# The pipeline of an adaLN block: its loop of five passes against nineteen bodies written out

## Chip, cores and metric

The kernel runs on one core of a Trainium2 chip. The metric is device time in microseconds (us) of one execution; for the kernel before three were timed, with a median of 753.84 us (753.83 to 755.56).

## What is computed

16 images (B) of 512 tokens by 128 channels, all in f32. Each goes through sliding-window attention with 16 heads of 8 channels, a window of 32 tokens to each side, and then a mixture of 8 experts, two of them chosen per token, with a shared expert beside them. Both halves are modulated by vectors that come from a condition.

```python
mod = (silu(c) @ wmod).reshape(16, 6, 1, -1)
sa, ca, ga, sb, cb, gb = (mod[:, i] for i in range(6))   # ga, gb kept away from 0 by 0.25
h = layernorm(x) * (1 + ca) + sa
x = x + ga * attention(h)          # q, k, v, softmax in a band of +-32, o
h = layernorm(x) * (1 + cb) + sb
x = x + gb * ffn(h)                # softmax router, top 2 of 8, silu(x w1) * (x w3) @ w2, and a shared expert
```

## The kernel before

**Tiling.** One image is the unit of work. Its tokens lie in the free dimension, 512 columns, and the 128 channels on the partitions. Products that need more precision than one fp32r pass gives are made from three matmuls of a high and a low part (`exact3`, L1157 to L1159). Attention takes 16 blocks of 32 queries; a block's four head groups are four matmuls of 96 keys (`scores`, L1214), then comes the row maximum on DVE (`maximum`, L883, tile nmx), the exponential with its sum on ACT (`probabilities`, L680, tile p), a transpose on DVE (`turn_p`, L900, tile pt) and the product with v on PE (`values`, L1237). Queries and keys reach the layout that `scores` needs by way of HBM: SP writes q_scr and k_scr and reads them back in two halves for each image (`load_half`, L320 for q, L328 for k), the second of which is needed at score block 8. The row sums go by way of r_scr (`spread_sums`, L350 and L354), and the router's weights by way of s_scr (`spread_scores`, L334 and L343, tile sbc, four transfers of 512 KB). The experts are nine rounds of two `exact3` products into ps_A and ps_B, a tanh on ACT (L723), two steps on DVE (L980 and L989), and the product with w2 (`down`, L1282); POOL makes the low parts of the experts' inputs (L494, L500).

**The pipeline.** Every engine (SP, POOL, ACT, DVE, PE) has one function `body(b, par)`, in which the steps of four images are interleaved by hand: image b's attention, image b+1's layer norm and projections, image b-1's output projection and router, and the experts of images b-2 and b-3. `has(b, back)` leaves out the steps of images that don't exist, at the two ends. `par` is b's parity and chooses buffers. There are 19 bodies, b from 0 to 18. The engines have no common barrier: each runs through its bodies by itself, and semaphores whose counts rise through the whole run tie them together.

`pipeline` (L232) issues the bodies. b = 0 to 3 and b = 14 to 18 are written out, with b an integer. b = 4 to 13 are a loop of five passes with two bodies in each, on every engine; b is a register expression there. In the loop each wait for a semaphore needs its count worked out by a register operation (REGISTER_ALU or ISA in the lists below, ALU_OP and FUSED_REGOPS in the trace), and every DMA to or from an image's own rows has an address from a register. At the end of a pass each engine adds to its counter and does a compare-and-branch (both at L236).

Of the kernel before, what the change touches and what calls it, by code (L numbers as in the profile page):

```python
# [28 lines left out]
B, S, D = 16, 512, 128  # L29
# [28 lines left out]
def build(nc, x, w13, w2, wqkv, wo, gate, bias, borow, cT, wmod, out):  # L58
    ctx = ExitStack()
    with ctx:  # L60
# [170 lines left out]

        def pipeline(eng, body):  # L232

            for b in range(4):
                body(b, b % 2)
            with eng.Fori(2, B // 2 - 1) as i:  # L236
                body(2 * i, 0)
                body(2 * i + 1, 1)
            for b in range(B - 2, B + 3):
                body(b, b % 2)  # L240

        def has(b, back, first=0):
# [17 lines left out]
        def _(sp):  # L260
# [120 lines left out]
            def body(b, par):  # L381
# [18 lines left out]
                if has(b, 1):  # L400
                    spread_scores(b - 1)

            pipeline(sp, body)
            sp.wait_ge(out_d, 16 * B + 16)


        @block.gpsimd
        def _(pool):
# [149 lines left out]
            def body(b, par):  # L558
# [45 lines left out]
                if has(b, 2):  # L604
# [3 lines left out]
                    scaled_low(b - 2, 7, par)  # L608

            pipeline(pool, body)  # L610


        @block.scalar
        def _(act):
# [119 lines left out]
            def body(b, par):  # L734
# [73 lines left out]
                if has(b, 2):  # L808
                    scaled_high(b - 2, 7, par)
                    scaled_high(b - 2, 8, par)  # L810

            pipeline(act, body)


# [627 lines left out]
```

## Time and profile before

| | |
|---|---|
| median of 3 runs | 753.84 us (753.83 to 755.56) |
| profiled execution | 756.55 us |
| its span, first to last instruction | 754.7 us |
| mean granted clock of TensorE over the span | 0.908 |
| PE busy | 672.0 us, 89% |
| ACT busy | 611.9 us, 81% |
| DVE busy | 580.9 us, 77% |
| POOL busy | 540.7 us, 72% |
| queue of the kernel's own DMAs (q1) | 62.8% of 16 engines |
| instruction queues (q8, q14) | 24 and 72 packets |

The busy shares are of the span and can lie over each other. The granted clock is a share of 2.4 GHz, and it stands either at 1.0 or at 0.5. The profiled execution took 2.7 us more than the median of the timed ones; sums in what follows are made against its own time.

### The profile page before, as it was taken

Reading aid. Unit: us, or ns where it says so; the run is one execution under the profiler, and the core shown is the slowest. Engines: PE = TensorE matmul, PEld = TensorE weight load, DVE = VectorE, ACT = ScalarE, POOL = GpSimd, SP = SyncE. Lnnn points to the kernel's source line nnn. Section 1 sums busy time; section 2 is a strip of 40 time slices with the busy share of each in tenths; the row PEclk is TensorE's granted clock in tenths of the full one; section 3 lists DMA queues with packets and bytes.
Section 4 is the critical chain, followed back from the end, with each engine's and each line's share of the span. In section 5 each row is a group of like instructions: output and inputs, shape, how many; then the busy total and the mean of one; then the engine's idle time right before and its main releaser. Section 6 shows DMA issues by size and latency. Waiting matters only on the chain.

```text
span 754.7 us, 20381 instructions
## 1 busy us (share of the span) xinstructions
PE 672.0 (89%) x5934; PEld 566.4 (75%) x5934; DVE 580.9 (77%) x1541; ACT 611.9 (81%) x2602; POOL 540.7 (72%) x564
## 2 busy tenths in 40 slices
PE   2278889989999889998899979998999999989886
PEld 1167677878888768877788768877888888877665
DVE  5456667978899759986899858987799899886453
ACT  4287879988999869997799959997799999885432
POOL 4430417896888768895688858896688888778784
PEclk9655557999999989999799979999799999999999
DMA  4746686767776856778476846878567878624120
GB/s 145 188 104 169 175 206 176 183 190 178 213 189 183 214 163 172 211 196 213 117 184 197 215 139 174 210 188 202 128 189 192 211 196 220 185 45 146 30 102 15
DMA packets 193856, 127.48 MB, mean 169 GB/s; under 512 B 110640, under 2 KB 170848, under 8 KB 193632
## 3 DMA queue, kind: packets, MB, share of 16 engines
q1 hardware_dynamic: 193760, 126.50, 62.8%
q14 instruction: 72, 0.59, 0.2%
q8 instruction: 24, 0.39, 0.2%
HBM read 96.29 MB, written 30.17 MB: 168 GB/s over the span
## 4 chain that ended last, share of the span: by engine, by line
PE 48%; DMA 15%; issue 9%; SPq 8%; POOL 7%; ACT 6%; DVE 6%; DVEq 0%; POOLq 0%; ACTq 0%
PE ps_s L1214 11%; DMA k<-k_scr 10%; PE ps_Y L1282 9%; PE ps_O L1237 5%; SPq L320 4%; ACT p L680 4%; PE ps_A L1157 3%; DMA r_scr<-rst 3%; PE ps_A L1158 2%; PE ps_A L1159 2%; PE ps_B L1157 2%; PE ps_B L1158 2%; PE ps_B L1159 2%; POOL xl L500 2%; POOL xs L494 2%
## 5 line engine op out<-in xcount | busy, mean ns | idle before, releaser
L680 ACT ACTIVATE p<-ps_s,nmx 128x96 f32<-128x96 f32 x1024 | 333.4, 351 | 59.7 <-DVE nmx L883 47.1
L680 ACT ACTIVATION_READ_ACCUMULATOR p<-ps_s,nmx 128x1 f32 x1024 | 222.2, 217 | 0.0
L1214 PE MATMUL ps_s<-k,q 128*128 128x96 f32 x1024 | 170.9, 302 | 48.9 <-DMA k<-k_scr 25.8
L1214 PEld LDWEIGHTS ps_s<-k,q 128*128 128x128 f32 x1024 | 151.8, 215 | 76.9 <-ACT p L680 37.9
L883 DVE TENSOR_REDUCE nmx<-ps_s 128x4 f32<-128x384 f32 x256 | 138.2, 548 | 70.7 <-PE ps_s L1214 61.9
L500 POOL TENSOR_TENSOR xl<-xs,xh 128x512 fp32r<-128x512 f32 x128 | 163.5, 1283 | 28.2 <-ACT xh L702 27.3
L494 POOL TENSOR_TENSOR xs<-h,sbc 128x512 f32<-128x512 f32 x128 | 163.8, 1285 | 5.0 <-DMA sbc<-s_scr 4.7
L1282 PE MATMUL ps_Y<-w2s,g 128*128 128x128 f32 x1152 | 162.2, 289 | 0.6 <-DVE g L989 0.6
L1282 PEld LDWEIGHTS ps_Y<-w2s,g 128*128 128x128 f32 x1152 | 149.3, 200 | 5.1 <-DVE g L989 0.8
L900 DVE STREAM_TRANSPOSE pt<-p 128x384 f32<-128x384 f32 x256 | 135.9, 558 | 2.8 <-ACT p L680 1.1
L980 DVE SCALAR_TENSOR_TENSOR th<-th,ps_A 128x512 f32<-128x512 f32 x144 | 97.7, 678 | 46.7 <-ACT th L723 46.6
L723 ACT ACTIVATE th<-ps_A 128x512 f32<-128x512 f32 x144 | 87.9, 610 | 26.8 <-PE ps_A L1159 25.6
L989 DVE TENSOR_TENSOR g<-th,ps_B 128x512 f32<-128x512 f32 x144 | 98.1, 682 | 12.7 <-PE ps_Y L1282 6.6
L702 ACT ACTIVATE xh<-xs 128x512 fp32r<-128x512 f32 x128 | 81.3, 645 | 22.9 <-POOL xs L494 22.0
L1157 PE MATMUL ps_A<-xh,w13h 128*128 128x512 f32 x144 | 71.2, 494 | 6.6 <-DVE th L980 5.0
L1237 PE MATMUL ps_O<-pt,vd 128*32 128x96 f32 (+2 forms) x2304 | 66.6, 252 | 0.7 <-POOL vd L472 0.7
L472 POOL TENSOR_TENSOR vd<-vt,bmask 128x1024 f32<-128x1024 f32 x32 | 60.6, 1894 | 0.1
L1157 PE MATMUL ps_B<-xh,w13h 128*128 128x512 f32 x144 | 59.2, 411 | 0.2
L1237 PEld LDWEIGHTS ps_O<-pt,vd 128*32 128x32 f32 x2304 | 48.2, 116 | 14.3 <-issue 6.0
L1158 PE MATMUL ps_A<-xh,w13l 128*128 128x512 f32 x144 | 58.6, 407 | 0.0
L1159 PE MATMUL ps_A<-xl,w13h 128*128 128x512 f32 x144 | 58.5, 406 | 0.0
L1158 PE MATMUL ps_B<-xh,w13l 128*128 128x512 f32 x144 | 58.3, 405 | 0.0
(119 smaller groups left out, 935.8 us busy)
## 6 DMA issues: line engine op xcount, KB each, us to landing
sbc<-s_scr SPq DMA_DIRECT2D x64, 512.0 KB, 5.5
k<-k_scr SPq DMA_DIRECT2D x64, 384.0 KB
q<-q_scr SPq DMA_DIRECT2D x128, 96.0 KB
k<-k_scr SPq DMA_DIRECT2D x32, 336.0 KB
q_scr<-qh SPq DMA_DIRECT2D x32, 256.0 KB, 2.5
k_scr<-kh SPq DMA_DIRECT2D x32, 256.0 KB, 2.9
xt<-x SPq DMA_DIRECT2D x16, 256.0 KB, 6.0
q_scr<-ql SPq DMA_DIRECT2D x16, 256.0 KB, 2.5
```

Source lines behind the costliest of these rows:

```text
L494: nc.gpsimd.tensor_tensor(xs[:, n % 2], h2[:, par], sbc[:, n - 1], ALU.mult).then_inc(xs_d, 1)
L500: nc.gpsimd.tensor_tensor(xl[:, n % XRING], src, xh[:, n % XRING].bitcast(F32), ALU.subtract).then_inc(xl_d, 1)
L680: last = nc.scalar.activation(p[:, n % PRING, gg, :], ps_s[:, n % 2, MK * gg:MK * gg + MK], ACT.Exp, bias=nmx[:, n, gg:gg + 1], accum_out= ...
L883: nc.vector.tensor_reduce(nmx[:, n, :], ps_s[:, n % 2, 0:ACC].rearrange("p (g k) -> p g k", g=HG), AX.X, ALU.max, negate=True).then_inc(mx ...
L900: nc.vector.transpose(pt[:, n % TRING].rearrange("p g r q -> p (g r q)"), p[:, n % PRING].rearrange("p g k -> p (g k)")).then_inc(tr_d, 1)
L980: nc.vector.scalar_tensor_tensor(th[:, par], th[:, par], 1.0, ps["A"][:], ALU.add, ALU.mult).then_inc(v_d, 1)
L989: nc.vector.tensor_tensor(g[:, par], th[:, par], ps["B"][:], ALU.mult).then_inc(g_d, 1)
L1157: mm(dst, wh, xh, start=True, stop=False)
L1158: mm(dst, wl, xh, start=False, stop=False)
L1214: last = mm(ps_s[:, n % 2, MK * gg:MK * gg + MK], heads[:, h, gg, nl], k4[:, h, gg, :, MB * nl:MB * nl + MB], start=gg == 0, stop=gg == HG ...
L1237: last = mm(ps["O"][r, MB * n0:MB * n0 + MB * cnt], vd[:, kb, gg].rearrange("p j d -> p (j d)"), src, start=kb == 0 and run is runs[0], st ...
L1282: last = mm(ps["Y"][:, QB * a:QB * a + QB], g[:, par, QB * a:QB * a + QB], w2s[:, e, :], start=n == 0 and a == 0, stop=n == NX - 1, skip_g ...
```

## The change

`pipeline` becomes a plain loop at build time. The bodies 4 to 13 get an integer b like the others, so their waits have constant counts and their DMAs constant addresses, and the branches and register operations of the loop are gone. What each body computes and the order of its steps stay as they are.

```diff
         def pipeline(eng, body):

-            for b in range(4):
-                body(b, b % 2)
-            with eng.Fori(2, B // 2 - 1) as i:
-                body(2 * i, 0)
-                body(2 * i + 1, 1)
-            for b in range(B - 2, B + 3):
+            for b in range(B + 3):
                 body(b, b % 2)
```

The file is five lines shorter, so L883 of before is L878 in the changed one, and so on.

DVE at the end of the loop's second body, before (nmx, th, g, pt: the maximum, the two expert steps, the transposed probabilities):

```order
L900 STREAM_TRANSPOSE pt<-p 128x384 [waits pv_mm,exp_d] x3
L883 TENSOR_REDUCE nmx<-ps_s 128x4 [waits sc_mm]
L979 REGISTER_ALU
L980 SCALAR_TENSOR_TENSOR th<-th,ps_A 128x512 [waits th_d]
L900 STREAM_TRANSPOSE pt<-p 128x384 [waits pv_mm,exp_d]
L989 TENSOR_TENSOR g<-th,ps_B 128x512 [waits y_mm,v_d,b_mm]
L236 REGISTER_ALU
L236 COMPARE_AND_BRANCH
```

and at the head of the loop's first body, to which the branch goes:

```order
L236 ISA
L883 TENSOR_REDUCE nmx<-ps_s 128x4 [waits sc_mm]
L888 ISA
L891 RECIPROCAL rs<-acc 128x64 [waits rst_mm,exp_d]
L838 ISA
L842 BN_STATS l_st<-xt 128x6 [waits x_in]
L842 BN_STATS l_st<-xt 128x6 x3
L882 REGISTER_ALU
L883 TENSOR_REDUCE nmx<-ps_s 128x4 [waits sc_mm]
```

The same place in the changed kernel, the end of an odd body and the head of the next:

```order
L895 STREAM_TRANSPOSE pt<-p 128x384 [waits pv_mm,exp_d] x3
L878 TENSOR_REDUCE nmx<-ps_s 128x4 [waits sc_mm]
L975 SCALAR_TENSOR_TENSOR th<-th,ps_A 128x512 [waits th_d]
L895 STREAM_TRANSPOSE pt<-p 128x384 [waits pv_mm,exp_d]
L984 TENSOR_TENSOR g<-th,ps_B 128x512 [waits y_mm,v_d,b_mm]
L878 TENSOR_REDUCE nmx<-ps_s 128x4 [waits sc_mm]
L886 RECIPROCAL rs<-acc 128x64 [waits rst_mm,exp_d]
L837 BN_STATS l_st<-xt 128x6 [waits x_in]
L837 BN_STATS l_st<-xt 128x6 x3
L878 TENSOR_REDUCE nmx<-ps_s 128x4 [waits sc_mm]
```

The compute instructions are the same and in the same order. The branch, its addition and the register operations are gone, and the head of the next body stands right behind the end of the one before.

ACT at the end of the loop's second body, before (xh: an expert's input rounded; p: exponentials):

```order
L680 ACTIVATE p,acc<-ps_s,nmx 128x96 x3
L698 REGISTER_ALU
L702 ACTIVATE xh<-xs 128x512 [waits b_mm,xs_d]
L698 REGISTER_ALU
L702 ACTIVATE xh<-xs 128x512 [waits b_mm,xs_d]
L236 REGISTER_ALU
L236 COMPARE_AND_BRANCH
```

and in the changed kernel:

```order
L675 ACTIVATE p,acc<-ps_s,nmx 128x96 x3
L697 ACTIVATE xh<-xs 128x512 [waits b_mm,xs_d] x2
L675 ACTIVATE p,acc<-ps_s,nmx 128x96 [waits tr_d,mx_d]
L675 ACTIVATE p,acc<-ps_s,nmx 128x96 x3
L718 ACTIVATE th<-ps_A 128x512 [waits g_d,a_mm]
```

Here too the next body's exponentials follow without a branch.

## Rows read from the trace of the kernel before

**Rows 1.** The page: busy time of PE and others, and the granted clock by slices.

```profile
PE 672.0 (89%) x5934; PEld 566.4 (75%) x5934; DVE 580.9 (77%) x1541; ACT 611.9 (81%) x2602; POOL 540.7 (72%) x564
...
PEclk9655557999999989999799979999799999999999
```

**Rows 2.** Windows of bodies 3 to 14: start:end, length, busy us (x instructions), PEclk, DMA share, GB/s.

```profile
144.60:186.50 41.90, 39.50 (x375) 33.93 (x371) 35.22 (x96) 37.51 (x164) 33.13 (x35) 0.96 0.67 187
186.50:225.02 38.52, 38.16 (x374) 32.48 (x371) 35.05 (x96) 37.37 (x164) 33.41 (x35) 1.00 0.78 204
225.02:266.70 41.68, 38.50 (x371) 32.39 (x371) 35.48 (x96) 38.22 (x166) 33.38 (x35) 1.00 0.72 188
266.70:311.28 44.58, 41.44 (x371) 35.41 (x371) 34.77 (x95) 36.68 (x159) 32.54 (x35) 0.92 0.67 175
311.28:350.39 39.11, 38.06 (x374) 32.55 (x370) 34.94 (x96) 37.60 (x166) 33.10 (x35) 1.00 0.74 199
350.39:396.80 46.41, 42.17 (x375) 35.88 (x371) 35.35 (x96) 37.27 (x162) 33.14 (x35) 0.89 0.62 168
396.80:435.28 38.48, 38.09 (x374) 32.56 (x371) 34.92 (x96) 37.58 (x166) 33.09 (x35) 1.00 0.73 202
435.28:482.43 47.15, 42.84 (x374) 36.47 (x371) 35.63 (x96) 37.58 (x164) 33.47 (x35) 0.89 0.62 166
482.43:521.78 39.35, 38.00 (x370) 32.50 (x371) 34.71 (x96) 37.56 (x164) 32.77 (x35) 1.00 0.77 198
521.78:567.86 46.08, 42.39 (x374) 36.08 (x370) 35.33 (x96) 37.27 (x162) 33.15 (x35) 0.89 0.63 170
567.86:606.21 38.35, 38.10 (x375) 32.56 (x371) 34.91 (x96) 37.47 (x166) 33.09 (x35) 1.00 0.79 203
606.21:644.05 37.84, 37.84 (x374) 32.51 (x370) 34.98 (x96) 37.09 (x164) 33.08 (x35) 1.00 0.75 198
```

**Rows 3.** Records of line L236, 264 to 271 us: ns min/median/max, first and last start.

```profile
L236 DVEq COMPARE_BRANCH  x1: 63/63/63, 265.8 to 265.8; - x1
...
L236 ACTq COMPARE_BRANCH  x1: 45/45/45, 267.0 to 267.0; - x1
...
L236 DVEq FUSED_REGOPS  x1: 74/74/74, 268.6 to 268.6; - x1
L236 ACTq FUSED_REGOPS  x1: 59/59/59, 269.4 to 269.4; - x1
```

**Rows 4.** Timeline of DVE behind the third branch: start, us, instruction [idle before].

```profile
444.00 0.56 DVE L883 TENSOR_REDUCE nmx<-ps_s 128x4 f32<-128x384 f32 x1 [4.17 <-PE ps_s L1214]
```

**Rows 5.** Timeline of ACT behind the third branch.

```profile
441.32 0.34 ACT L680 ACTIVATE p<-ps_s,nmx 128x96 f32<-128x96 f32 x1 [4.59 <-issue]
```

**Rows 6.** Timeline of PE, in body 5 and behind the third branch.

```profile
248.62 0.65 PE L1214 MATMUL ps_s<-k,q 128*128 128x96 f32 x4 [2.53 <-DMA k<-k_scr]
...
442.77 1.09 PE L1214 MATMUL ps_s<-k,q 128*128 128x96 f32 x4 [3.15 <-ACT p L680]
```

**Rows 7.** Windows behind the first and the third branch, columns as in rows 2.

```profile
275.00:281.90 6.90, 6.79 (x24) 6.11 (x25) 4.91 (x9) 4.60 (x21) 4.92 (x6) 0.51 0.36 82
...
442.30:452.50 10.20, 9.30 (x35) 8.43 (x36) 6.86 (x17) 6.84 (x33) 5.42 (x8) 0.50 0.18 45
```

**Rows 8.** DMA queues, 275 to 600 us and then 606 to 644 us: packets, MB, share.

```profile
q14 instruction: 39, 0.32, 0.3%
...
q8 instruction: 3, 0.05, 0.6%
```

**Rows 9.** Timeline of SP in bodies 5 and 14: start, us, instruction.

```profile
226.86 1.76 SPq L343 DMA_DIRECT2D sbc<-s_scr  x4
...
236.99 0.57 SPq L354 DMA_DIRECT2D rt<-r_scr  x1
...
606.40 1.76 SPq L343 DMA_DIRECT2D sbc<-s_scr  x4
...
614.75 0.57 SPq L354 DMA_DIRECT2D rt<-r_scr  x1
```

## The prediction

> **What bounds the kernel now.** I read the page first, then a table of windows, one for each body of the pipeline (a body's window runs from the first score matmul of one image, L1214, to that of the next), then the branch records, the timeline behind a branch, the clock, and last the DMA queues.
>
> The page has PE at 89% of the span, and a granted clock with dips to 7 and 8 tenths that come back again and again in the middle of the run [rows 1]. Those dips are what the reader should take from it: something regular interrupts TensorE there.
>
> The windows say what. Bodies 4 to 13 are the five passes of the loop; body 3 and body 14 are written out. Body 14 lasts 37.84 us with PE busy 37.84, so it is bound by PE at the full clock. The odd bodies of the loop last 38.35 to 41.68 us with PE busy 38.00 to 38.50. The even bodies 6, 8, 10 and 12 last 44.58, 46.41, 47.15 and 46.08 us, at a mean clock of 0.92 or 0.89 [rows 2]. Body 4 is even too and lasts 38.52 us, at clock 1.00: it is the one even body of the loop that is entered from the code above and not over the branch back. So the long bodies are those behind a taken branch, not the even ones as such.
>
> The records of line L236 show the gap. At the end of the first pass DVE's compare-and-branch starts at 265.8 us and takes 63 ns, and its next record, the first instruction of the loop's body, starts at 268.6; ACT's pair is 267.0 and 269.4 [rows 3]. Nothing is waited for there: these are register operations. Behind the third branch ACT stands 4.59 us with the releaser "issue", DVE stands 4.17 us once more before its second maximum, and PE then waits 3.15 us for ACT's exponentials [rows 4 to 6]. DVE's 4.17 is put down to PE's scores, but ACT's own late start shows how little was moving. Right behind that the granted clock is 0.50, the lower of its two levels (1.2 of 2.4 GHz), for 10.20 us, and 0.51 for 6.90 us behind the first branch [rows 7]. TensorE had been standing before each of these stretches.
>
> Where the instructions come from is in the DMA view. Between 275 and 600 us the queue named instruction q14 has 39 packets, and PE's kind of queue, q8, has no row at all. In body 14 there are three packets of q8, 0.6% of 16 engines over 38 us, which is 3.6 us or 1.2 us for each packet [rows 8]. I read this as: the two bodies of the loop stay loaded for PE, while DVE and ACT must have theirs brought back after a branch, and stand until it has come.
>
> **The change, part by part.**
>
> *The four taken branches go.* The loop has five passes and so four branches back, one just ahead of the start of each of the bodies 6, 8, 10 and 12; the fifth falls through. The four bodies behind them sum to 44.58 + 46.41 + 47.15 + 46.08 = 184.22 us. A body without a branch before it costs PE's work plus PE's waits. PE's work: bodies 4, 5, 7, 9, 11, 13 and 14 have 38.16, 38.50, 38.06, 38.09, 38.00, 38.10 and 37.84 us, mean 38.11. PE's waits, window less busy: 0.36, 3.18, 1.05, 0.39, 1.35, 0.25 and 0.00, mean 0.94 [rows 2]. Together 39.05, four times 156.2. Gain 28.0 us. It divides into PE's idle time, 3.14 + 4.24 + 4.31 + 3.69 = 15.4 us, less 4 x 0.94, and PE's longer busy time, 41.44 + 42.17 + 42.84 + 42.39 less 4 x 38.11 = 16.4 us, which is matmuls at half the clock.
>
> That the price lies behind the branch and not in it can be weighed against a rule. The branch record itself is 63 ns on DVE and 45 ns on ACT [rows 3]. The Trainium skill, "Advanced Engine Details and Errata", Control Flow Timing, gives a compare-and-branch about 108 ns and names no other cost; by that rule alone four branches are worth 0.4 us on an engine, and the time would stay near 753.4 us. The Trainium skill, "Runtime: NRT & Kernel Launch", Instruction fetch mechanics, says the other thing: a taken branch to a target outside the loaded window has to fetch it, and the engine stands. The trace agrees with the second, by 2.4 and 2.7 us between branch and next record.
>
> *The other six bodies of the loop* sum to 38.52 + 41.68 + 39.11 + 38.48 + 39.35 + 38.35 = 235.49 us; six times 39.05 is 234.3. Gain 1.2 us. There is no direct gain in them.
>
> *Register operations and separate waits go.* In the loop each wait count is made by a register operation before the instruction; with constants it isn't. The loop's odd bodies need 38.00 to 38.50 us of PE, body 14 without register operations 37.84 [rows 2]. Some tenths for a body at most, and PE's queue runs ahead of PE. I put it at nothing; the 0.27 us between 38.11 and 37.84 in ten bodies, 2.7 us, is kept for the low end. Below nothing it can't well be, since no instruction is added. On SP the same holds: issues of its DMAs with constant addresses are of the same length in body 14 (1.76 us for four of sbc) as in body 5 [rows 9].
>
> *What is added is code to be brought in.* Eight more bodies of instructions on every engine. For PE the loop had none to bring between 275 and 600 us; written out it has three blocks a body, as body 14 shows, some 30 in ten bodies. In body 14 the blocks land and PE is busy 37.84 of 37.84 us, so I cost them at nothing: what hides them is that they are fetched ahead. Their traffic is 0.6% of the DMA engines.
>
> **Sum.** 419.7 us of loop become 390.5: 29.2 us less. The profiled execution took 756.55 us (span 754.7 and 1.85 around it), so 727.3 by its own account. The median of the runs is 753.84, 2.7 less than the profiled one, and gives 724.6. I take the middle, **726.0 us**.
>
> **What is late next** is the second half of k. In body 5 PE waits 2.53 us at score block 8 for k from k_scr [rows 6]. SP had put the four transfers of sbc at 226.86, the row sums could be read back only at 236.99, 10.1 us later, and k was issued behind that. In body 14 the same steps are 606.40 and 614.75, 8.4 us, and PE waits for nothing [rows 2, 9]. The order on SP isn't changed, so this wait stays and decides how much of the gain is kept.
>
> **The rivals.**
> 1. *The k wait settles at its worst.* Bodies 4 and 5, the only two full ones in a row at full clock without a branch before either, average 40.10 us. Ten of them are 401.0: a gain of 18.7 and 737.9 us from the profiled time, 735.1 from the median. For it: bodies 3 and 5 both have it, at 41.9 and 41.68 [rows 2]. Against: bodies 9, 13 and 14 hardly have it. Chance 0.22.
> 2. *No k wait at all.* Ten bodies like body 14, 378.4 us: a gain of 41.3, 712.5 to 715.3 us. Only one body in seven was like that. Chance 0.08.
> 3. *Nothing changes*, because the branch costs only its own record, or because the stall behind it is one that the pipeline has at the turn of each pair of bodies for another reason. Four times 63 ns less, 753.6 us. Body 4 and body 14, even and without a stall, speak against it. Chance 0.03.
> 4. *Slower: PE must wait for its own blocks.* If PE came to the end of a block before the next had landed, each of 30 blocks would cost it the 1.2 us that a packet takes, 36 us, or more in a full DMA queue, and the stops would pull the clock down as they do now: 756.5 - 29.2 + 36 = 763 us. It decides from 1.0 us a block. For it: on PE the loop is the better form as it stands, no fetch in 325 us. Against: three blocks in body 14 with no idle time. Chance 0.03.
>
> **The numbers.** My own forecast has 0.64. The range must take in rival 1 and most of the likely case's spread: its ends are 737.9, where the k wait is at its worst, and 715.3, where it is gone, measured from the median. So 715 to 738. A difference of 0.3%, 2.3 us, is what a measurement of this kernel can tell from none; the forecast and rivals 1 and 2 are all far beyond it. Faster 0.94, same 0.03, slower 0.03.
>
> **What the profile of the changed kernel would show.** No record of line L236's branch. No idle time of ACT or DVE put down to issue in the middle of the run, and no stretch at clock 0.50 between 180 and 700 us, so slices of 9 in the PEclk row. Bodies 4 to 13 of 38 to 41 us each, the odd and the even alike. A mean clock up from 0.908, PE's busy time down by some 16 us to 656, 90% of the new span. Some 24 more packets in q8. What would prove me wrong: bodies 6, 8, 10 and 12 still over 44 us; PE idle for issue at even distances; or waits for k of over 3 us, which would say that DMA has become the bound.

## The result, and the profile after

The changed kernel takes 748.7 us (median of 20 runs, 741.6 to 756.3) and the kernel before 755.2 (median of 20, 746.7 to 761.3). The ratio is 0.9917, 95% interval [0.989, 0.9945]: a gain of some 6.5 us in place of 29. The profiled executions are 746.85 us after and 756.55 before, spans 745.1 and 754.7, 9.6 us apart. Ratios here and below leave out executions over 1.5% slower than the fastest of their kernel, medians keep them (three of the changed kernel's 20, and one of 2311 us among the six of the kernel that spreads 16 KB over 16 engines).

From the page of the changed kernel, beside [rows 1]; the last two lines are the instruction queues (packets, MB, share), which were 24 and 72 packets:

```profile
PE 660.5 (89%) x5934; PEld 558.9 (75%) x5934; DVE 581.2 (78%) x1541; ACT 613.0 (82%) x2602; POOL 541.2 (73%) x564
...
PEclk9996557999989999999999999999999999999999
...
q8 instruction: 47, 0.77, 0.5%
q14 instruction: 53, 0.43, 0.2%
```

The dips in the middle of PEclk are gone at this resolution, and so is every record of the branch. q8, the queue that fills when PE is written out, has 23 packets more. (11868 matmuls and weight loads and 321 semaphore instructions of PE over 47 packets are 259 each; in what follows a block is one 16 KB packet of q8, by this estimate some 256 instructions.) Here are the windows of bodies 4 to 14, with the columns of [rows 2]:

```profile
186.73:230.08 43.35, 41.07 (x375) 35.51 (x371) 35.21 (x96) 37.64 (x164) 33.07 (x35) 0.92 0.69 181
230.08:268.85 38.77, 37.89 (x375) 32.50 (x371) 35.07 (x96) 37.41 (x164) 33.10 (x35) 1.00 0.78 201
268.85:308.89 40.04, 38.15 (x375) 32.40 (x371) 35.17 (x96) 37.45 (x164) 33.07 (x35) 1.00 0.71 196
308.89:348.26 39.37, 38.19 (x374) 32.51 (x370) 35.07 (x96) 37.62 (x164) 33.13 (x35) 1.00 0.76 199
348.26:388.72 40.46, 37.99 (x375) 32.51 (x371) 35.75 (x96) 38.02 (x166) 33.69 (x35) 1.00 0.72 194
388.72:428.20 39.48, 37.90 (x370) 32.50 (x370) 34.52 (x95) 36.94 (x161) 32.59 (x35) 1.00 0.76 198
428.20:467.24 39.04, 37.90 (x374) 32.50 (x370) 35.09 (x96) 37.41 (x164) 33.09 (x35) 1.00 0.79 201
467.24:509.83 42.59, 39.48 (x374) 33.91 (x370) 35.19 (x96) 37.51 (x164) 33.15 (x35) 0.96 0.71 184
509.83:551.85 42.02, 39.79 (x375) 34.08 (x371) 35.22 (x97) 37.64 (x164) 33.11 (x35) 0.96 0.72 186
551.85:591.39 39.54, 37.96 (x374) 32.50 (x371) 35.61 (x96) 37.94 (x166) 33.66 (x35) 1.00 0.76 198
591.39:633.14 41.75, 39.50 (x370) 33.99 (x370) 34.68 (x96) 37.20 (x161) 32.62 (x35) 0.96 0.65 180
```

The even bodies are no longer the long ones. But the ten bodies 4 to 13 sum to 404.7 us against 419.7 before and 390.5 in the forecast, and body 14, which was written out in both kernels, went from 37.84 to 41.75. The four bodies behind a branch lost 22.7 us (184.22 before, 161.56 now); bodies 4, 5, 7, 9, 11 and 13 went from 235.49 to 243.10 us and gave a third of that back.

PE's waits, first in the changed kernel, 186.7 to 591.4 us, then in the kernel before, 186.5 to 606.2 us (who waited for whom: us, times, longest):

```profile
PE ps_s L1209 <- DMA k<-k_scr: 17.6, 11, 3.1
PE ps_B L1152 <- DVE g L984: 0.2, 1, 0.2
```

```profile
PE ps_s L1214 <- ACT p L680: 13.7, 8, 3.1
PE ps_s L1214 <- DMA k<-k_scr: 6.7, 9, 2.5
PE ps_M L1247 <- DVE rs L891: 1.5, 3, 0.5
```

The waits for ACT behind a branch, 13.7 us, are gone as forecast. The waits for k went from 6.7 to 17.6 us: one at score block 8 of each body, and a short one at the start of body 9. The four bodies with the longest waits (4, 11, 12 and 14, 2.1 to 3.1 us) are those with a mean clock under 1.00. The half clock that [rows 7] showed behind the branches stands behind these waits too, here in bodies 14 and 4:

```profile
616.00:619.00 3.00, 3.00 (x14) 2.81 (x13) 2.35 (x5) 2.94 (x14) 3.00 (x4) 0.51 0.91 348
...
209.50:216.00 6.50, 6.50 (x28) 6.21 (x29) 3.81 (x7) 3.93 (x19) 6.50 (x6) 0.50 0.54 207
```

How a wait for k comes about can be followed on SP. In body 14 of the changed kernel (beside body 14 in [rows 9]):

```profile
588.60 0.32 SPq L329 DMA_DIRECT2D s_scr<-smT  x1
593.12 1.75 SPq L338 DMA_DIRECT2D sbc<-s_scr  x4
596.33 1.44 SPq L345 DMA_DIRECT2D r_scr<-rst  x2
600.93 0.57 SPq L349 DMA_DIRECT2D rt<-r_scr  x1
...
604.87 3.05 SPq L323 DMA_DIRECT2D k<-k_scr  x3
```

PE then stands at score block 8:

```profile
614.04 0.65 PE L1209 MATMUL ps_s<-k,q 128*128 128x96 f32 x4 [2.25 <-DMA k<-k_scr]
```

In the kernel before, the two rows of body 14 that [rows 9] lacks are:

```profile
603.94 0.34 SPq L334 DMA_DIRECT2D s_scr<-smT  x1
...
611.15 1.46 SPq L350 DMA_DIRECT2D r_scr<-rst  x2
```

From the s_scr write (588.60) to sbc are 4.5 us, before 2.5. The r_scr write goes out 4.94 us into the body in both kernels, since it waits for ACT's row sums. It takes 4.6 us from there to rt, before 3.6, so rt goes out at 9.5 us into the body instead of 8.5 and k at 13.5 instead of 12.5. The changed kernel's PE goes on at 22.6 us, having stood for 2.25; before, it passed the same block at 20.35 us without a wait. So k's own landing was later by more than the 1.0 us that its issue had lost.

### The profile page after: what moved, and what is told of

Read it like the earlier page. It is cut to its first block, busy times and chain, and to the rows that moved or that the text cites. A ratio compares the mean times of both kernels' runs of the same rounds, so it can differ in the third digit from the quotient of the medians.

```text
span 745.1 us, 18977 instructions
## 1 busy us (share of the span) xinstructions
PE 660.5 (89%) x5934; PEld 558.9 (75%) x5934; DVE 581.2 (78%) x1541; ACT 613.0 (82%) x2602; POOL 541.2 (73%) x564
## 4 chain that ended last, share of the span: by engine, by line
PE 42%; DMA 22%; SPq 13%; POOL 8%; issue 6%; ACT 5%; DVE 3%; POOLq 0%; DVEq 0%; ACTq 0%
DMA k<-k_scr 15%; PE ps_s L1209 11%; PE ps_Y L1277 10%; SPq L315 8%; DMA r_scr<-rst 6%; PE ps_O L1232 5%; ACT p L675 4%; SPq L323 3%; PE ps_A L1152 3%; POOL xl L495 3%; POOL xs L489 2%; PE ps_M L1260 2%; PE ps_A L1153 2%; PE ps_A L1154 2%; PE ps_B L1152 2%
## 5 line engine op out<-in xcount | busy, mean ns | idle before, releaser
L675 ACT ACTIVATION_READ_ACCUMULATOR p<-ps_s,nmx 128x1 f32 x1024 | 215.7, 211 | 0.0
L1209 PE MATMUL ps_s<-k,q 128*128 128x96 f32 x1024 | 167.2, 297 | 54.1 <-DMA k<-k_scr 42.2
L1209 PEld LDWEIGHTS ps_s<-k,q 128*128 128x128 f32 x1024 | 147.6, 210 | 81.4 <-DMA k<-k_scr 50.2
L878 DVE TENSOR_REDUCE nmx<-ps_s 128x4 f32<-128x384 f32 x256 | 138.0, 548 | 67.4 <-PE ps_s L1209 64.0
L1232 PE MATMUL ps_O<-pt,vd 128*32 128x96 f32 (+2 forms) x2304 | 64.9, 247 | 0.0
L1154 PE MATMUL ps_B<-xl,w13h 128*128 128x512 f32 x144 | 57.2, 397 | 0.0
```

What stands on the lines that cost most here:

```text
L675: last = nc.scalar.activation(p[:, n % PRING, gg, :], ps_s[:, n % 2, MK * gg:MK * gg + MK], ACT.Exp, bias=nmx[:, n, gg:gg + 1], accum_out= ...
L878: nc.vector.tensor_reduce(nmx[:, n, :], ps_s[:, n % 2, 0:ACC].rearrange("p (g k) -> p g k", g=HG), AX.X, ALU.max, negate=True).then_inc(mx ...
L1154: return mm(dst, wh, xl, start=False, stop=True)
L1209: last = mm(ps_s[:, n % 2, MK * gg:MK * gg + MK], heads[:, h, gg, nl], k4[:, h, gg, :, MB * nl:MB * nl + MB], start=gg == 0, stop=gg == HG ...
L1232: last = mm(ps["O"][r, MB * n0:MB * n0 + MB * cnt], vd[:, kb, gg].rearrange("p j d -> p (j d)"), src, start=kb == 0 and run is runs[0], st ...
```

## Experiments

All ratios are to the kernel before, which ran on the same chip beside them, with 95% intervals. The first question is which engine's code made the difference. `pipeline` got a switch, so that each engine could keep the old loop or be written out:

```diff
-        def pipeline(eng, body):
+        def pipeline(eng, body, loop=False):
...
-            pipeline(pe, body)
+            pipeline(pe, body, loop=True)
```

**PE alone in the loop** (the diff above; it is the kernel "with PE alone in the loop" below, and the one that the others are held against).

> PE alone keeps the loop of five passes, the other four engines are written out. Theory A (the 16 KB instruction blocks that PE fetches in written-out code, 1.0 to 1.3 us each and three per body, hold up the short transfers s_scr, r_scr and k): no such block between 260 and 600 us, the k waits of PE fall back from a mean of 2.0 us per body to about 1, and the time is 5 us or more below the changed kernel's 748.7, that is a ratio to the kernel before of 0.985 or less. Theory B (the chain over sbc, r_scr and k is just as long as PE's work once no engine stalls, whatever is fetched): same as the changed kernel, ratio 0.99 to 0.993, k waits still 2 us. If PE's branch costs something of its own, the even bodies are longer than the odd ones.

726.3 us, ratio 0.9599 [0.9548, 0.9651]. First the windows of its bodies 6, 9 and 13 and the sum over bodies 6 to 13; then PE's waits in bodies 4 to 13, and q8 on its page:

```profile
269.53:308.25 38.72, 37.88 (x375) 32.50 (x371) 35.05 (x96) 37.35 (x163) 32.99 (x35) 1.00 0.76 201
...
385.91:423.84 37.93, 37.91 (x375) 32.51 (x371) 34.98 (x96) 37.15 (x164) 33.08 (x35) 1.00 0.77 205
...
539.73:577.36 37.63, 37.63 (x375) 32.60 (x371) 35.10 (x96) 37.04 (x164) 33.04 (x35) 1.00 0.76 207
sum 307.83, PE 303.19 PEld 260.15 DVE 280.55 ACT 298.41 POOL 264.41; mean PE 37.90 PEld 32.52 DVE 35.07 ACT 37.30 POOL 33.05
```

```profile
PE ps_s L1218 <- DMA k<-k_scr: 8.8, 8, 2.3
```

```profile
q8 instruction: 24, 0.39, 0.2%
```

The eight bodies 6 to 13 take 307.8 us, 38.5 each, where the changed kernel takes 322.5. The waits for k are half of what they were, and of their 8.8 us 4.2 lie in bodies 4 and 5, the pass in which q8 still has packets. This is the size that the prediction had given for the whole change: 30 us less than the 756.7 of its own comparison. Writing PE out as well costs 22 us (748.7 against 726.3), 24 by the ratios.

**PE alone written out** (`loop=True` for the other four).

> PE alone is written out, the other four engines keep the loop. Theory A: the stalls of DVE and ACT behind the branch stay and PE's blocks come in addition, so slower than the kernel before by 2 to 6 us, ratio 1.003 to 1.008. Theory B: the time of the kernel before, ratio 0.998 to 1.002. In both the even bodies 6, 8, 10 and 12 keep their 44 us and more.

767.0 us, ratio 1.015 [1.0088, 1.0212]: slower than before by 10 us, more than the 2 to 6 expected. Its bodies 6, 8, 10 and 12 keep the stall (two are shown) and sum to 182.05 us, no more than before; the six bodies without a branch ahead of them take 244.5 us against 235.49. So PE's blocks cost where the kernel before had little else to wait for. q8 has the packets of the changed kernel:

```profile
267.27:313.58 46.31, 42.74 (x375) 36.36 (x371) 35.32 (x96) 37.26 (x162) 33.14 (x35) 0.89 0.64 170
...
527.44:573.39 45.95, 41.17 (x375) 34.95 (x371) 35.33 (x96) 37.27 (x162) 33.14 (x35) 0.93 0.64 171
```

```profile
q8 instruction: 47, 0.77, 0.4%
```

**DVE and ACT alone written out** (`loop=True` for PE, POOL and SP).

> DVE and ACT alone are written out, PE, POOL and SP keep the loop. If the stall of these two behind the branch is all that the loop cost, and PE's blocks all that writing it out cost, the time is that of the kernel in which PE alone loops: 722 to 730 us, ratio 0.955 to 0.965. If POOL's or SP's branch costs something too, it lies above 730.

734.1 us, ratio 0.9721 [0.9685, 0.9757]. Above 730: the loops of DVE and ACT together are some 21 us of the loop's price, and 8 to 9 lie in the loops of POOL and SP. Which of these two it is was not tested.

**A PE loop too long to stay loaded.** PE keeps the looped form with its register waits, but in two passes of four bodies:

```diff
-            with eng.Fori(2, B // 2 - 1) as i:
-                body(2 * i, 0)
-                body(2 * i + 1, 1)
-            for b in range(B - 2, B + 3):
+            with eng.Fori(1, 3) as i:
+                for k in range(4):
+                    body(4 * i + k, k % 2)
+            for b in range(12, B + 3):
```

> As the kernel in which PE alone loops (726.3 us), but PE's loop has two passes of four bodies (4 to 11) in place of five of two; bodies 12 and 13 are written out on PE. Four bodies are some 12 blocks of 256 instructions. Theory A (fetching PE's blocks is what costs): they don't stay loaded, q8 has 40 packets or more, and the time goes back to 742 to 752 us, of which up to 5 us may be the one branch back if its target must be fetched. Theory C (it is the looped form of the code, with its register waits, that runs better on PE): 724 to 730 us, and so whatever q8 shows.

742.2 us, ratio 0.9764 [0.9717, 0.9811]. q8 goes up to 50 packets, and by the ratios half of the loss (0.0165 of 0.0318) comes back with them. PE's one taken branch now shows a wait of its own ("issue"), at the first score matmul of body 8:

```profile
q8 instruction: 50, 0.82, 0.5%
```

```profile
PE ps_s L1218 <- DMA k<-k_scr: 11.2, 7, 3.0
PE ps_s L1218 <- issue: 3.1, 1, 3.1
```

The looped form alone would have given 724 to 730 us, so it is not what runs better; with the packets half of the loss is back. Why not all of it is, although there are as many packets as in the changed kernel, is not shown by this run. The next three show that the same packets can cost as little.

**Where the blocks fall.** Waits that are long fulfilled, ahead of PE's body 0, push each block to another place in the bodies:

```diff
             project_v(0)
+            for _ in range(256):
+                pe.wait_ge(w_in, 112)
```

(By the trace 128 of them make 64 instructions, 256 make 128, 384 make 192.)

> The changed kernel with 64 more wait instructions on PE ahead of body 0, where PE waits for k anyway. Nothing else moves, but each 16 KB instruction block (256 instructions) is fetched 64 instructions earlier, some 3.3 us of a body of 39: from 12.4, 27.2 and 38.2 us after a body's start to 9.1, 23.9 and 34.9. Theory A1 (a block costs when it meets the last packets of a short transfer of the chain s_scr, r_scr, k): the block leaves the landing of s_scr (-2.3 to +1 us around a body's start), and the time moves by 3 us or more from 748.7, most likely down to 735 to 745. Theory A2 (a block costs the same wherever it falls): 746 to 751.

> As the kernel with 64, with 128 more waits: blocks at 5.8, 20.6 and 31.6 us after a body's start. Theory A1: the second block now meets the landing of k (20 to 23 us), so this is among the slower ones, 745 to 755. Theory A2: 746 to 751.

> As the kernel with 64, with 192 more waits: blocks at 2.5, 17.3 and 28.4 us after a body's start, in the middle of the sbc transfers and of the loads of q and k, away from the landings of s_scr and of k. Theory A1: the fastest of the four places, 725 to 740. Theory A2: 746 to 751.

740.9 us, 0.9823 [0.9779, 0.9868]; 739.9 us, 0.9782 [0.9732, 0.9831]; 752.1 us, 0.9947 [0.9917, 0.9977]. PE's waits for k in the three, 186 to 600 us:

```profile
PE ps_s L1209 <- DMA k<-k_scr: 10.5, 8, 2.0
```

```profile
PE ps_s L1209 <- DMA k<-k_scr: 12.9, 11, 2.9
```

```profile
PE ps_s L1209 <- DMA k<-k_scr: 15.2, 12, 3.1
```

The place does matter: 12 us between kernels that do the same work, each with 48 packets in q8. "A block costs the same wherever it falls" had asked for 746 to 751 us in all three, and fails clearly for the first two. The guess of which place is best was wrong for 128 and for 192. For 64 and 192 it had taken the blocks to be clear of the way from the s_scr write to sbc, and they are not: of the eleven stretches from the s_scr write to sbc ahead of bodies 4 to 14, a q8 packet runs in all 11 in the changed kernel, in 8 with 64, in none with 128 and in 9 with 192. Yet 64 and 128 are not told apart by their intervals, and both are slower than PE alone in the loop (0.9599). So there are better and worse places, but meeting the landing of s_scr is not what decides.

With the long loop these are five kernels in which PE fetches throughout, at 0.9764, 0.9782, 0.9823, 0.9917 and 0.9947. Their distance to 0.9599 puts the price of the fetch between 0.0165 and 0.0348, some 12 to 26 us of 755; the changed kernel has one of the dear places.

**A block imitated.** To the kernel with PE alone in the loop SP gets one more transfer in each body, just ahead of the s_scr write, that nothing reads: once as one packet of 16372 bytes, once as 16 packets of 1 KB.

```diff
                 if has(b, 1):
+                    sp.dma_start(dump[b:b + 1], w13.rearrange("p e k n -> (p e k n)").unsqueeze(0)[:, 0:4093]).then_inc(dmp_d, 16)
                     spread_scores(b - 1)
```

> The kernel in which PE alone loops (726.3 us) with one more DMA in each body on SP, just ahead of the s_scr write: 4093 contiguous f32 from HBM to HBM, which is one packet of 16372 bytes on one DMA engine, the size of a PE instruction block. Nothing reads it. Theory A1 (one long packet on one DMA engine holds up the landing of the short s_scr write that is spread over all 16): the time from the s_scr write to the first sbc transfer grows from 2.8 to 3.5 us or more, the k waits of PE with it, and the time is 733 to 742 us, at least 5 us above the kernel with the same bytes spread. Theory B2 (it is only the added load, or the layout of the code, that matters): the same as the spread one.

> The same kernel and the same place, with 4096 contiguous f32, which are 16 packets of 1 KB, one on each engine. Theories A1 and B2 both: SP's one issue more and 16 KB of load, 725 to 731 us.

729.2 us, 0.9627 [0.9582, 0.9673], and 730.2 us, 0.9635 [0.9584, 0.9686]. The same pair with 7177 and 7168 numbers:

> As the kernel with one packet of 16 KB per body ahead of the s_scr write (729.2 us), with 7177 f32, 28.7 KB in one packet, which at the rate seen (16 KB in 0.67 us) takes 1.2 us, as long as a PE block. Theory A1 (a packet that outlasts the others on its DMA engine holds up s_scr's landing): 734 to 742 us, and the time from the s_scr write to sbc grows by 0.4 us or more against the spread pair. Otherwise, if one packet on SP's queue is not what a block does: within 2 us of the spread one.

> The same bytes in 16 packets of 1.8 KB, one on each engine: 728 to 732 us under either theory.

734.3 us, 0.9667 [0.9621, 0.9713], and 733.0 us, 0.9657 [0.9608, 0.9707]. No difference within either pair; the longer packet took 1.1 us, as long as a PE block. One long packet on SP's queue, at this place, is not what a PE block does to the chain. These runs also say how far a single trace can be trusted: PE's waits for k from 186 to 600 us are 7.5 us with the one packet of 16 KB and 13.7 with the spread one, in executions of 728.0 and 730.1 us.

What the traces show of it is this. SP's waits for the two short writes, whole run, first in the changed kernel, then with PE alone in the loop:

```profile
SPq L349 <- DMA r_scr<-rst: 48.9, 16, 3.9
SPq L338 <- DMA s_scr<-smT: 44.0, 16, 4.2
```

```profile
SPq L358 <- DMA r_scr<-rst: 43.3, 16, 4.3
SPq L347 <- DMA s_scr<-smT: 36.9, 16, 3.6
```

Both are longer with PE's blocks, by 7.1 and 5.6 us, 0.8 us in a body together. But the sum of the two, 92.9 and 80.2 us here, is 88.5 in the spread 16 KB kernel, where PE's loop is kept, and 81.8 in the kernel shifted by 128, where PE is written out. In the stretches ahead of bodies 4 to 14 of ten profiled executions with SP's order unchanged (but for the extra transfer in two), 110 in all, the way from the s_scr write to sbc takes 3.59 us where a q8 packet runs in it (48) and 2.92 where none does (62). That is a coincidence in time, and the imitation didn't bring it about.

Where the time goes in the chain can be told from the starts on SP, counted from PE's first score matmul, as means of bodies 4 to 13 (changed kernel, then PE alone in the loop): sbc 1.24 and 0.62 us, r_scr write 4.93 and 4.93, rt 9.77 and 9.26, last load of k 15.60 and 14.67. The later sbc does not put the r_scr write off; half of the 0.9 us arises between that write and rt, half between rt and the last load of k. With the shift by 128 the starts are those of the loop (k at 14.63), and PE, where it waits at block 8, goes on 6.9 us behind the last load of k, in the other two kernels 6.6. So in one kernel k is issued late, and in the other it seems to land late. What a block does to the transfers stays open.

**The wait for k itself.** Three kernels change SP's order. First the load of the second half ahead of the row sums, all engines written out:

```diff
-                if has(b, 1):
-                    spread_sums(b - 1)
                 if has(b, 0, 1):
                     load_half(b, 1)
+                if has(b, 1):
+                    spread_sums(b - 1)
```

> The changed kernel with SP's load of the second half of q and k (load_half(b, 1)) put ahead of spread_sums(b - 1). Theory B: k lands some 4 to 6 us earlier, PE's waits for it go, and if nothing else is late the ten bodies fall to 38.1 us, about 725 to 732 us, ratio 0.96 to 0.97; the row sums rt come 5 us later, and if scale_o on DVE and attn_out on PE then wait for them, part or all of it is given back, 745 us or more. Theory A alone (short transfers held up by instruction blocks) gives little, since rt is then held up in k's place.

836.4 us, 1.1056 [1.0999, 1.1112]. The wait for k is gone, and PE waits in attn_out for DVE, which stands ahead of scale_o. The profile puts that wait down to issue; what scale_o needs there by the code are the row sums, which now come after q and k:

```profile
PE ps_M L1252 <- DVE vt L873: 56.4, 8, 8.6
...
DVE o L904 <- issue: 62.6, 8, 9.4
```

Then the split of sbc: two of its four transfers go behind the load of k (a wait for the late ones ahead of the next s_scr write comes with it). All engines are written out:

```diff
                 if has(b, 0, 1):
                     load_half(b, 1)
+                if has(b, 2):
+                    spread_more(b - 2, (2, 3))
...
-                    spread_scores(b - 1)
+                    spread_scores(b - 1, (0, 1))
```

> The changed kernel with two of the four 512 KB transfers of sbc (those of experts 4 to 7) issued after load_half(b, 1) of the next body instead of ahead of the row sums. Theory B: the r_scr write no longer stands behind 2 MB but behind 1 MB, so rt and k come 2 to 3 us earlier, PE's waits for k go, and the time falls to 725 to 735 us, ratio 0.96 to 0.975. Theory A alone: a fall of 2 us for the whole run at most. If the late transfers hold up the experts on POOL, PE waits for xl instead.

718.9 us, 0.9509 [0.9449, 0.957], better than expected. PE's blocks are still fetched here, and its waits for k, 186 to 600 us, are well under the 17.6 of the changed kernel:

```profile
q8 instruction: 47, 0.77, 0.5%
...
PE ps_s L1220 <- DMA k<-k_scr: 6.9, 9, 2.2
```

The same split with PE alone in the loop:

> PE alone loops, and two of the four sbc transfers go behind the load of k (718.9 us with PE written out). If PE's blocks and the 2 MB of sbc act on the same wait for k and the split has already taken most of it, the two don't add: 712 to 718 us. If they were independent the sum would be 718.9 - 22.4 = 696.5, which PE's own work of 38.1 us for each body does not allow.

715.6 us, 0.944 [0.9396, 0.9484], the lowest median of all. With the split, PE's blocks cost 0.0069, 3 to 5 us and within the two intervals, where they cost 0.0318 without it. This speaks for a price that goes by way of the wait for k: with k issued earlier the same 23 blocks hardly cost. PE's waits for k, 186 to 600 us:

```profile
PE ps_s L1229 <- DMA k<-k_scr: 3.8, 6, 1.4
```

The split in the kernel before, all engines in the loop:

> The kernel before (all five engines in the loop) with the split of sbc alone. The stalls behind the four branches stay, 28 us by my sum, and the waits for k in the odd bodies go, some 1 us in each of five: 745 to 752 us, ratio 0.985 to 0.995. If the branch stalls were hidden once k is early, it would fall below 735.

743.4 us, 0.9795 [0.9748, 0.9843], some 2 us below the range. It keeps its waits behind the branch, and loses most of those for k (6.7 us without the split):

```profile
PE ps_s L1229 <- ACT p L695: 12.0, 6, 2.9
PE ps_s L1229 <- DMA k<-k_scr: 1.8, 2, 1.5
```

Last, PE alone in the loop with three of the four transfers behind the load of k:

> PE alone loops, and three of the four sbc transfers, not two, go behind the load of k (two: 715.6 us). If PE still waits for k there, rt and k come another 1 us earlier and the time falls to 711 to 715 us; if POOL then waits for the weights of experts 2 and 3, which it multiplies early in the body, it rises to 720 or more.

853.7 us, 1.1231 [1.1177, 1.1286]. Three late transfers are one too many: POOL waits for the weights of experts 2 and 3 (66.5 us in eight waits, 186 to 600 us) ahead of making hl, and PE's projection waits for hl:

```profile
PE ps_M L1172 <- POOL hl L479: 59.8, 8, 8.4
```

## Why the prediction was wrong

- **The four taken branches**: right as a mechanism. The waits for ACT behind them, 13.7 us, and the half clock behind those are gone in the changed kernel, and with the branches gone on the other four engines and PE's code kept loaded the time is 726.3 us (forecast 726.0). That this agrees so closely is in part luck: by its ratio it would be 723.6 of the forecast's 753.84, and of the loop's price only some 21 us belong to DVE and ACT, to which the prediction had put all of its 28, and 8 to 9 to POOL and SP. That the price lies behind the branch, and not in its 45 to 63 ns, stands: the long loop shows 3.1 us of it on PE too. The Trainium skill, "Runtime: NRT & Kernel Launch", Instruction fetch mechanics, has the rule that a taken branch to code outside the loaded window stalls the engine; the trace of the long loop agrees with it, by these 3.1 us.
- **"What is added is code to be brought in", costed at nothing**: this is the step that failed. It measured 22 us (748.7 against 726.3), and 10 us on top of the old loop (767.0 against 756.7). The argument was that PE isn't idle in body 14 with three blocks. It looked for the cost at PE's own instruction stream, and there it is indeed nothing: PE has no wait for issue in bodies 4 to 13 of the changed kernel. The cost shows in PE's waits for k, and nearly vanishes with the split that brings k forward. How a block makes k late is not shown.
- **The waits for k, 0.94 us a body**, were too small for the same reason. PE's idle time in bodies 4 to 13 (window less busy) is 18.3 us, 1.8 a body, where the forecast had 9.4 for the ten, and its busy time is 5.2 us over 381.1, for the half clock behind the longer waits. Together that is the 14.2 us between 404.7 and 390.5. The mean of 0.94 came from seven bodies, four of which (7, 9, 11 and 13) lay in passes where PE fetched nothing. For such bodies it was fair: with PE alone in the loop bodies 6 to 13 have 0.58. Bodies 3, 4, 5 and 14 of the kernel before had three q8 packets each and 2.40, 0.36, 3.18 and 0.00 us of idle time, a mean of 1.5; the argument rested on the last of them alone.
- **Rival 1** (k at its worst, 735 to 738 us) had the right place, and a time 9 us too low (737.9 against 746.85 in the profiled execution). The ten bodies took 3.7 us more than its 401.0, and it left the rest as it was, where body 14 lost 3.9 us and the run behind it 1.3.
- **Rival 4** (slower through PE's own blocks) had the right cause and the wrong path. It asked for 1.0 us a block with PE idle for issue. The blocks, 23 more, cost about that each, by way of k, and took back three quarters of the gain. It also counted 30 blocks where the signs to look for count 24; with 24 its own 1.2 us a block come to 29 us, the whole gain and no more.
- **The range.** Its low end, 715.3 us, is the profiled time less 41.3 and not, as the prediction says, measured from the median, which gives 712.5. The result lies beyond the other end, so nothing hangs on it.
- **The signs to look for**: no branch records, 23 of some 24 packets, a mean clock of 0.943 up from 0.908, and no dips at even distances came as said. Stretches at half clock between 180 and 700 us did come, behind the waits for k. Bodies 4, 11 and 12 lasted 42.0 to 43.4 us and not 38 to 41, and PE's busy time is 660.5 us and not 656. Waits "of over 3 us", set as the sign that DMA had become the bound, came once (3.11 us, body 11); nine of 0.9 to 2.3 us at the same score block did the same.

## What to carry to other kernels

Code that an engine fetches is traffic, and its price need not show at that engine as a wait for issue: before unrolling, look at which transfers the kernel's bound engine waits for, and how much slack their chain has. Loop and straight code can be chosen engine by engine; here PE does better in its loop of two bodies, which left no fetch in the trace, and DVE and ACT, tested together, do better written out. A wait measured in bodies where an engine fetches nothing says little of the wait where it does, and a chain with no slack should be given some first: with the split of sbc the same unrolling is worth 2.9% (0.9509 against 0.9795) and not 0.8%.

## Not expected of the hardware

PE's loop of two bodies left no q8 packet from 275 to 600 us of the kernel before, while one of four bodies brought 26 there and 50 in the run. With PE's code moved by 128 instructions against the data the kernel takes 739.9 us, by 192 it takes 752.1, with nothing else touched. And the mean granted clock says little of a single run here: of the changed kernel's executions, those at 0.979 to 0.981 took 747.3 to 748.8 us and of three at 0.919 two took 745.5 and 746.0, the third 749.0.
